# A fused LayerNorm and attention kernel on one core: the tensor engine's work goes by pairs of tiles, each with one burst of small matmuls, padded with empty instructions to 768

## What is computed

```python
def proj(W, b):
    y = jnp.einsum('nse,fe->nsf', x, W) + b
    return y.reshape(n, s, h, d).transpose(0, 2, 1, 3)      # n, 16 heads, 2048 tokens, 32
scores = jnp.einsum('nqhd,nkhd->nhqk', Q, K) * scale        # q and k run over the heads
attn = softmax(scores, axis=-1)
out = jnp.einsum('nhql,nlhd->nqhd', attn, V).reshape(n, s, e)
return jnp.einsum('nse,fe->nsf', out, Wo) + bo
...
x = x + _layernorm(_L0_attn_ref(_layernorm(x, axis=-1), ...), axis=-1)
x = x + _layernorm(_L0_ffn_ref(_layernorm(x, axis=-1), ...), axis=-1)
```

## Time and profile before

| what | value |
|---|---|
| runs | 1688.67, 1690.04, 1692.35 us (median 1690.04) |
| profiled execution, first to last instruction | 1686.3 us |
| PE / DVE / POOL / ACT busy | 98% / 78% / 76% / 51% of the span |
| granted clock of PE, mean | 0.994 |
| instructions in the trace | 55468, of these 22550 matmuls and as many weight loads |

### The profile page before, as it was taken

How to read it: one execution, slowest core, us unless ns; L and a number is a source line. 1 busy time by engine, 2 the same in 40 slices (tenths; PEclk the granted TensorE clock), 3 DMA queues, 4 the chain that set the end, 5 groups by cost and what they waited for, 6 DMA issues and landing times.

```text
span 1686.3 us, 55468 instructions
## 1 busy us (share of the span) xinstructions
PE 1657.2 (98%) x22550; PEld 1320.8 (78%) x22550; DVE 1309.6 (78%) x2455; ACT 855.4 (51%) x1730; POOL 1285.2 (76%) x1303
## 2 busy tenths in 40 slices
PE   8999999999999999999999999999999999999994
PEld 6777887877878778788877877887887887787873
DVE  7687877877877877778778778778787787787777
ACT  4355455555544544554555555445445555555453
POOL 5577877877877778778778778787787787787777
PEclk9999999999999999999999999999999999999997
DMA  7666666666666666666666666666666676666553
GB/s 252 173 172 184 176 169 171 182 178 174 166 188 170 175 175 183 172 179 179 172 170 179 180 175 166 184 175 171 173 186 170 173 187 171 173 168 189 155 139 88
DMA packets 388635, 293.46 MB, mean 174 GB/s; under 512 B 296854, under 2 KB 296854, under 8 KB 388380
## 3 DMA queue, kind: packets, MB, share of 16 engines
q1 hardware_dynamic: 345552, 223.02, 49.8%
q10 hardware_dynamic: 42828, 66.90, 13.2%
HBM read 155.46 MB, written 67.24 MB: 132 GB/s over the span
## 4 chain that ended last, share of the span: by engine, by line
PE 95%; DVE 2%; issue 1%; ACT 1%; POOL 1%; ACTq 1%; DMA 0%; DVEq 0%
PE ps_k L1080 8%; PE ps_y L1160 7%; PE ps_y L1161 7%; PE ps_v L1080 7%; PE ps_y L1164 7%; PE ps_v L1083 7%; PE ps_v L1081 7%; PE ps_q L1080 7%; PE ps_k L1081 7%; PE ps_q L1083 7%; PE ps_k L1083 7%; PE ps_q L1081 7%; PE ps_s L1121 6%; PE ps_o L1140 5%; ACTq L943 0%
## 5 line engine op out<-in xcount | busy, mean ns | idle before, releaser
L910 ACT ACTIVATE q_sb<-ps_q,mr 128x512 f32<-128x512 f32 x127 | 87.5, 689 | 537.6 <-issue 537.6
L403 POOL TENSOR_TENSOR z<-z,b_row 128x512 f32<-128x512 f32 x124 | 187.5, 1533 | 222.7 <-DVE z L679 222.7
L605 DVE STREAM_TRANSPOSE qT<-q_sb 128x512 f32<-128x512 f32 x128 | 137.6, 1075 | 107.4 <-ACT q_sb L910 106.9
L1080 PE MATMUL ps_k<-wk_hi,xT_hi 128*128 128x512 f32 x504 | 212.2, 421 | 0.3 <-issue 0.3
L1160 PE MATMUL ps_y<-wo_hi,oT_hi 128*128 128x512 f32 x504 | 200.3, 397 | 2.1 <-ACT oT_hi L926 1.9
L1161 PE MATMUL ps_y<-wo_lo,oT_hi 128*128 128x512 f32 x504 | 199.7, 396 | 0.0
L1080 PE MATMUL ps_q<-wq_hi,xT_hi 128*128 128x512 f32 x504 | 199.5, 396 | 0.0
L1081 PE MATMUL ps_k<-wk_lo,xT_hi 128*128 128x512 f32 x504 | 199.2, 395 | 0.4 <-issue 0.4
L1080 PE MATMUL ps_v<-wv_hi,xT_hi 128*128 128x512 f32 x504 | 199.4, 396 | 0.0
L383 POOL TENSOR_TENSOR x_t<-x_t,mr_row 128x512 f32<-128x512 f32 x126 | 195.7, 1553 | 4.4 <-ACT mr_row L1005 4.4
L1081 PE MATMUL ps_q<-wq_lo,xT_hi 128*128 128x512 f32 x504 | 198.9, 395 | 0.0
(11 more groups left out here) (189 smaller groups left out, 3721.0 us busy)
## 6 DMA issues: line engine op xcount, KB each, us to landing
x_in<-in_xa SPq DMA_DIRECT2D x64, 512.0 KB, 4.9
x_t<-in_xt SPq DMA_DIRECT2D x64, 512.0 KB, 4.8
k_bd<-kT SPq DMA_DIRECT2D x512, 64.0 KB, 2.4
v_d<-v_tok ACTq DMA_DIRECT2D x128, 256.0 KB, 2.2
v_key<-v_d SPq DMA_DIRECT2D x128, 256.0 KB, 3.9
res<-in_xr SPq DMA_DIRECT2D x64, 512.0 KB, 4.9
p_bd<-pT ACTq DMA_DIRECT2D x508, 64.0 KB, 2.3
out<-o_sb SPq DMA_DIRECT2D x62, 512.0 KB, 2.9
```

Of the source, the lines that this page charges most:

```text
L403: nc.gpsimd.tensor_tensor(z[:, j, :], z[:, j, :], b_row[:, :], ALU.add).then_inc(z_done, 1)
L605: nc.vector.transpose(qT[t % 2][:, :, :].rearrange("p n h -> p h n"), q_sb[:, :].rearrange("p (h d) -> p h d", d=D)).then_inc(qT_done, 1)
L1080: nc.tensor.matmul(ps, x_hi[:, e, :], w_hi[:, e, :], start=e == 0, stop=False)
```

## The change

PE's loop now goes by pairs of tiles (a, b). A pair begins with one burst: the mixings of two tiles (a - 4, b - 4), then the scores of the next two (a - 2, b - 2), 256 small matmul records in a row. Then come eight groups of big matmuls. For this the scores and the mixings of two tiles stand beside each other in the two halves of ps_s and ps_o (`half_of`), `top`, `total` and `z` are doubled, and the engines wait for both tiles (`both`). The mixing of a tile now comes one burst after its scores, its output another half pair later, and the normalisations A and B run three pairs behind (v = p - 3) and C four (u = p - 4). In the start 78 empty instructions are added, in every pair four times 14, in the end five times 21. The loops of the other engines are written by pairs too, and the ends are reordered: some additions move from POOL to DVE, and four outputs use other PSUM banks.

```diff
-        top = sb("top", [P, 16, 2])
-        total = sb("total", [P, 16, 2])
+        top = [sb(f"top{i}", [P, 16, 2]) for i in range(2)]
+        total = [sb(f"total{i}", [P, 16, 2]) for i in range(2)]
...
-        z = sb("z", [P, 2, E])
+        z = sb("z", [P, 2, 2, E])
...
+        def half_of(t):
+            return slice(E // 2 * (t % 2), E // 2 * (t % 2) + E // 2)
+
+        def both(t):
+            return (t | 1) + 1
+
+        def mixed_in(t):
+            return ps_s[:, :, half_of(0)] if t == NT - 1 else ps_o[:, :, half_of(t)]
+
+        def o_turned(t):
+            return (xT_hi[0], xT_lo[0]) if t == END + 1 else (oT_hi[t % 2], oT_lo[t % 2])
+
+        def mixed_by(t):
+            return NT - 1 if t == NT - 2 else both(t)
...
-                if t:
+                if t % 2 == 0 and t:
                     pe.wait_ge(sub_done, t)
+                to = ps_s[:, :, half_of(t)]
...
-                else:
+                if t == 0:
                     pe.wait_ge(kT_done, 2)
                     pe.wait_ge(q_put, 2)
+                elif t == NT - 1:
+                    pe.wait_ge(sub_done, NT)
+                elif t % 2 == 0:
+                    pe.wait_ge(olo_done, t)
+                to = mixed_in(t)
                 for a in range(4):
                     for g in range(4):
...
+            def spare(n):
+                for _ in range(n):
+                    nc.tensor.nop(hint='pad', nofuse=True)
...
             rows(1, range(4), ps_y)
             queries(1)
             values(0)
-            scores(0)
             values(1)
             keys(2)
+            scores(0)
             scores(1)
             queries(2)
             values(2)
-            mixed(0)
-            scores(2)
             keys(3)
             queries(3)
-            mixed(1)
-            output(0)
+            spare(78)
             values(3)
-            output(1)
-            for s in range(4, NT - 2):
-                scores(s - 1)
-                mixed(s - 2)
-                keys(s)
-                queries(s)
-                values(s)
-                output(s - 2)
+            for p in range(2, NV - 1):
+                a, b = 2 * p, 2 * p + 1
+                mixed(a - 4)
+                mixed(b - 4)
+                scores(a - 2)
+                scores(b - 2)
+                keys(a)
+                queries(a)
+                spare(14)
+                values(a)
+                spare(14)
+                keys(b)
+                spare(14)
+                output(a - 4)
+                spare(14)
+                queries(b)
+                values(b)
+                output(b - 4)
+            scores(NT - 4)
             scores(NT - 3)
+            mixed(NT - 6)
+            mixed(NT - 5)
+            keys(NT - 2)
+            spare(21)
+            queries(NT - 2)
+            spare(21)
+            values(NT - 2)
+            spare(21)
+            keys(NT - 1)
+            spare(21)
+            queries(NT - 1)
+            spare(21)
+            output(NT - 6)
+            scores(NT - 2)
+            scores(NT - 1)
             mixed(NT - 4)
-            keys(NT - 2)
-            queries(NT - 2)
-            values(NT - 2)
-            keys(NT - 1)
-            scores(NT - 2)
             mixed(NT - 3)
-            queries(NT - 1)
+            values(NT - 1)
+            output(NT - 5)
             output(NT - 4)
-            scores(NT - 1)
-            values(NT - 1)
+            output(NT - 3)
             mixed(NT - 2)
-            output(NT - 3)
+            mixed(NT - 1)
             output(NT - 2)
-            mixed(NT - 1)
             output(NT - 1)
```

More of the change, by code:

```diff
@@ new lines, in _ @@
+            y_in(NT - 7)
+            y_stats(NT - 7)
+            less_top(NT - 4)
+            less_top(NT - 3)
+            weigh(NT - 4)
+            k_turn(NT - 2)
+            p_turn(NT - 4)
+            z_stats(NV - 5)
+            weigh(NT - 3)
+            x1_stats(NV - 4)
+            q_turn(NT - 2)
+            out_add(NV - 5, 0)
+            out_add(NV - 5, 1)
+            k_turn(NT - 1)
+            p_turn(NT - 3)
+            o_low(NT - 6)
+            z_add(NV - 4, 0)
+            o_low(NT - 5)
@@ L793, in _ @@
+            z_add(NV - 4, 1)
+            q_turn(NT - 1)
+            z_stats(NV - 4)
+            less_top(NT - 2)
+            y_in(NT - 6)
+            y_stats(NT - 6)
+            less_top(NT - 1)
+            weigh(NT - 2)
+            o_low(END)
+            o_low(END + 1)
+            p_turn(NT - 2)
             y_in(NT - 5)
-            less_top(NT - 3)
             y_stats(NT - 5)
-            weigh(NT - 3)
-            k_turn(NT - 2)
-            p_turn(NT - 3)
-            z_stats(NV - 4)
@@ L800, in _ @@
[L800 to L808 removed]
+            weigh(NT - 1)
             y_in(END)
[L810 removed]
             end_sums("A", END)
+            p_turn(NT - 1)
             end_moments("A", END)
[L813 to L815 removed]
```

467 lines of the change are left out of this document (227 added, 240 removed).

## The result

The changed kernel took 1712.4 us in the median of four runs (1711.5 to 1717.8), the kernel before 1691.2 us beside it. The ratio is 1.0129 with a 95% interval of 1.0103 to 1.0156: slower. I had forecast 1670.0 us, at most 1695, and faster with a chance of 0.79. The prediction is wrong in sign and outside its range. The profiled execution has a span of 1716.0 us against 1686.3, so 29.7 us are to be found.

What follows compares the result with a forecast made beforehand. PE's own pace was taken to bound the loop. Loop -18, pauses -1.5, start -1.5 and end +1 gave -20 us: span 1666.3, median 1670.0 us; own range 1660 to 1679, overall 1659 to 1695, faster at 0.79.

Steps and rivals of the forecast that it cites:

- The burst of a pair: PE's loop: two tiles sharing one burst take 25.37 us instead of 25.66, saving 18 us over 61 pairs.
- The pauses: Rare pauses in PE's bursts, 2.2 us in all, go or come every pair at fixed packet borders: -1.5 us, -2.2 to +7.
- the first rival: The burst outruns its instruction packets and stands 1.0 us in every pair: 1731 us, slower; chance 0.11.
- The start: Before the loop: the 1.82 us stop ahead of the first burst should go: -1.5 us, between -2 and +1.
- The end: Last two mixings share a burst and wait for both softmaxes, PE stopping about 3.7 us: +1 us, -4 to +5.
- the 22 us that I had named as the sign of a wrong cost: Kernel's end: PE's last output more than 22 us before the end would mean the end was costed wrongly.
- The empty instructions: Four groups of 14 per pair on PE's sequencer, 0.051 us each, hidden by queued big matmuls: nothing, upper end 76 us.
- ACT's round: ACT's work per pair, 0.9 us left in 25.4, costed at nothing; as rival bound, 1690 to 1715 us, chance 0.14.
- the 4 us in hand: Slack of the longest chain feeding the burst: DMAs land 2.3 us after issue at 20.9, needed at 25.4.

Runs made afterwards that it cites:

- e12: Changed kernel with 70 instead of 78 empty instructions at the start and the four 512 KB transfers of a pair issued behind the end of keys(a): 1677.8 us, ratio 0.9933.
- e16: As e12 but 72 empty instructions at the start, and at the end GpSimd's roots for the last two tiles ahead of the z additions: 1682.9 us, ratio 0.9952.
- e6: Kernel before the change, with 14 empty instructions behind queries(s) and 14 behind values(s) in each tile of its loop: 1688.6 us, ratio 0.9985.
- e5: As e1, with 78 instead of 14 empty instructions in each of the four groups of the loop: 2512.4 us.
- e1: Changed kernel with 70 instead of 78 empty instructions ahead of values(3), borders eight instructions later in the program: 1706.4 us, ratio 1.0093.
- e2: Changed kernel with 62 instead of 78 empty instructions ahead of values(3), borders sixteen instructions later: 1771.8 us, ratio 1.0480.
- e3: Changed kernel with 86 instead of 78 empty instructions ahead of values(3), borders eight instructions earlier: 1769.9 us, ratio 1.0467.
- e14: Changed kernel, still with 78 empty instructions at the start, the four 512 KB transfers of a pair issued behind the end of keys(a): 1709.3 us, ratio 1.0109.
- e10: As e1, with the three 512 KB transfers for res, x_in and out moved behind keys_out(b) and the store of x_d: 1788.8 us, ratio 1.0589.

## Why the prediction was wrong, step by step

- *The burst of a pair*, 25.37 us: right. Undisturbed pairs took 25.32 to 25.34 us; the third and the fourth group of 64 were as fast as the first, as I had taken. e12 shows the gain when little takes it back: 25.40 us a pair in the mean.
- *The pauses*, -1.5 us, between -2.2 and +7: this is the step that failed. The old pauses went (-2), but the stops at the fixed borders cost +40 us. Its place in the text is the sentence of the first rival, "then the next border comes 256 instructions on, fetched long before, and the third meets big matmuls again". I counted big matmuls behind a border as safety. They are only as much safety as they take time: between the second border (1.4 us behind the first mixing) and the third (5.2 us) lie 3.8 us, and the next packet was usable only 4.1 to 4.5 us after the second border was passed. My bound of +7 took its size from a pause of 0.12 us in a burst behind which 256 instructions took far longer; nothing bounds the mechanism there.
- *The first rival* had the right mechanism, but I gave it 0.11 because I set its condition wrongly: "the point from which it decides is that a border is met after the burst has begun". It decides at any 256 instructions passed in less than about 4.1 us, wherever they begin. I reckoned with 2.3 us for a packet, the landing of a p_bd at that time; from the passing of a border to a usable packet it was 4.1 us or more, of which the time on the DMA engines is the 1 us that I had worked out. That its 1.0 us a pair is near the measured 0.65 is luck: it set 2.3 us against the 1.3 us of 256 instructions within the burst, where it was 4.3 against 3.8 behind it. What it said of the border's place, within 30 instructions of the burst's beginning, was right (23). The Trainium skill (Runtime: NRT & Kernel Launch, section Instruction fetch mechanics) has the price of a border mostly hidden, dispatch being slower than the fill. It is, for big matmuls: 256 instructions of them are 30 us. For a burst of 64x32x64 products it is not, and the measurement decides.
- *The start*, -1.5 us: -0.5, but the first pair +7, by the same two borders, here with 1.9 and 3.0 us.
- *The end*, +1 us, between -4 and +5: +5, at the edge. The last output stands 27.1 us before the end, beyond the 22 us that I had named as the sign of a wrong cost. The stop of PE that I had laid out as 3.7 us was 1.5 (before the last mixing). What I had not costed is POOL, which holds the chain for 17.9 us of the end instead of 5.9. Its order is not the cause (e16); whether it is the amount of its work no run shows.
- *The empty instructions*, nothing: right for groups of 14 (e6), though the size was too small: 71 ns, not 51. "By it the cost is nothing" went too far: that the sequencer alone handles an empty instruction doesn't make it free, as e5 shows.
- *ACT's round*: fell. PE waited for no engine in the loop. But "they land 2.3 us later" was wrong, in the changed kernel they landed 5.7 us later, and the 4 us in hand were nearly gone.

What is shown and what isn't: the border's place as the cause of the stops, by e1, e2, e3 and e14; that loads in flight make a packet late, by e10 against e12. In e1 itself the same holds from pair to pair: in the 19 pairs in which the DMA engines were over 30% busy from 2.0 to 0.5 us ahead of the burst, stop 1 is 0.76 us, in the other 39 it is 0.15. That this traffic is p_bd, k_bd and the rows behind the four loads is inferred from their landings; no run took these transfers away one by one. The cause of the longer end stays open.

## What to carry to other kernels

Count instructions, not only time: before a stretch of short matmuls is made longer, find the shortest time in which any 256 successive instructions of that engine pass, and compare it with the time from a border to the next usable packet (here 4.1 to 4.5 us). Where a loop is padded to whole packets the borders stay put, so their place must be chosen, on both sides of the burst. Keep large loads out of the microseconds before it, since the packet queues behind them.

## What the runs showed of the hardware

- A packet of instructions is delayed by data on the core's DMA engines. With 1.5 MB in flight it started 2.2 us later (-1.2 to +1.0 us, e12 and e10).
- From the border within the burst to the first matmul behind the next one it took 4.3 us in the changed kernel (medians of 58 pairs): 1.6 until the packet started on its DMA queue, 1.1 there, and 1.6 from its landing to the matmul. The last part was 1.4 us in e2 and e10.
- Empty instructions started 71 ns apart on PE's sequencer; this was hidden for groups of 14 and not for groups of 78.
- Behind a stop of 2.88 us in e5, PE's granted clock was 0.52 for 3.5 us, the level of 1.2 GHz, and the big matmuls started 0.43 us apart instead of 0.234; then 1.00 again.
- TensorE took the 256 matmul records of a burst (128 small products of 64 x 32 x 64) in 2.6 us, 10 ns from start to start, with no slowing from the first group of 64 to the fourth.
